# A Mamba block and a butterfly FFN on one core: state products in row halves, a decay formed from sums, and new orders in the first and the last unit

## The reference, cut to what matters

```python
x = x + ssm(layernorm(x), in_proj_w, conv_w, conv_b, x_proj_w, A_log, D, out_proj_w)
x = x + ffn(layernorm(x), W_exp, b_exp, up_weights, up_bias, down_weights, W_con, b_con, down_bias)

def ssm(x, ...):
    x_inner, z = split(x @ in_proj_w.T)              # 2 x 512 channels
    x_conv = silu(causal_conv4(x_inner) + conv_b)
    x_dbl = x_conv @ x_proj_w.T                      # 1 + 16 + 16 columns
    delta = softplus(x_dbl[..., 0]); B, C = x_dbl[..., 1:17], x_dbl[..., 17:]
    A = -exp(A_log)                                  # 16 rates
    # over the tokens t, for each of the 512 channels d and 16 states n
    h = h * exp(delta_t * A) + x_t[d] * delta_t * B_t[n];   y_t[d] = sum_n h[d, n] * C_t[n]
    return ((y + x_conv * D) * silu(z)) @ out_proj_w.T

def ffn(x, ...):                                     # 256 -> 1024 -> 256
    h = butterfly(x @ W_exp + b_exp, up_weights)     # 10 stages of 2x2 mixes
    h = butterfly(gelu(h + up_bias), down_weights)
    return h @ W_con + b_con + down_bias
```

## Time and profile before

| | |
|---|---|
| median of three runs | 568.49 us |
| lowest, highest | 566.38, 570.36 us |
| the profiled execution's own time | 569.59 us |
| its span, first to last instruction | 567.9 us |
| mean granted TensorE clock | 0.966 |
| TensorE matmuls busy | 528.9 us, 93% |
| VectorE, ScalarE, GpSimd busy | 72%, 54%, 19% |

### The profile page before, as it was taken

How to read it: one execution, slowest core, us unless ns; L and a number is a source line. 1 busy time by engine, 2 the same in 40 slices (tenths; PEclk the granted TensorE clock), 3 DMA queues, 4 the chain that set the end, 5 groups by cost and what they waited for, 6 DMA issues and landing times.

```text
span 567.9 us, 8152 instructions
## 1 busy us (share of the span) xinstructions
PE 528.9 (93%) x2996; PEld 430.3 (76%) x2996; DVE 409.6 (72%) x860; ACT 306.1 (54%) x526; POOL 109.5 (19%) x96
## 2 busy tenths in 40 slices
PE   3998899888999999999999999999999999699896
PEld 3766676776897779887888778877888788578886
DVE  4859999587983799468966799379946894575532
ACT  2876883865239622874268623962287417431342
POOL 4042100230201301050103120130105021411110
PEclk9986979799999999999999999999999999799999
DMA  8542311200012001210112001200021002100011
GB/s 244 97 27 3 80 35 38 76 2 2 23 52 74 4 2 48 66 39 2 37 41 74 0 9 68 71 8 1 5 73 38 0 2 74 41 1 0 6 34 37
DMA packets 42619, 21.75 MB, mean 38 GB/s; under 512 B 26419, under 2 KB 41011, under 8 KB 42580
## 3 DMA queue, kind: packets, MB, share of 16 engines
q1 hardware_dynamic: 39940, 17.57, 13.0%
q10 hardware_dynamic: 2640, 3.67, 2.3%
HBM read 16.78 MB, written 4.46 MB: 37 GB/s over the span
## 4 chain that ended last, share of the span: by engine, by line
PE 48%; DVE 20%; issue 12%; ACT 9%; SPq 6%; POOL 3%; DMA 0%; DVEq 0%; ACTq 0%; POOLq 0%
PE wide L711 12%; PE acc L844 9%; PE wide L833 7%; SPq L420 5%; PE wide L822 4%; DVE xc L1552 2%; DVE xc L1555 2%; POOL x1b_xn L598 2%; DVE state L1516 2%; DVE hid_low L1429 2%; PE wide L804 2%; PE small L731 2%; PE wide L811 2%; DVE xc L1412 2%; ACT L1054 2%
## 5 line engine op out<-in xcount | busy, mean ns | idle before, releaser
L1054 ACT ACTIVATE hid_f<-wide,bias_up 128x512 f32<-128x512 f32 x64 | 44.0, 687 | 162.0 <-PE wide L833 161.6
L1412 DVE SCALAR_TENSOR_TENSOR xc<-xi,taps,xc 128x512 f32<-128x512 f32 x96 | 87.0, 911 | 4.0 <-ACT xc L1085 1.7
L844 PE MATMUL acc<-w_down_high,hid_high 128*128 128x256 f32 x256 | 73.2, 286 | 5.6 <-DVE hid_low L1429 5.4
L844 PE MATMUL acc<-w_down_high,hid_low 128*128 128x256 f32 x256 | 71.9, 281 | 0.0
L844 PE MATMUL acc<-w_down_low,hid_high 128*128 128x256 f32 x256 | 71.9, 281 | 0.0
L1429 DVE TENSOR_TENSOR hid_low<-hid_f,hid_high 128x512 fp32r<-128x512 f32 x64 | 46.3, 725 | 29.8 <-ACT hid_high L1163 29.2
L833 PE MATMUL wide<-xnT_ln2T_high,w_up_high 128*128 128x512 f32 x128 | 55.4, 432 | 3.4 <-DVE xnT_ln2T_low L1423 1.8
L522 POOL TENSOR_TENSOR rstd<-var_eps,minus_half 128x4 f32<-128x4 f32 x16 | 19.1, 1192 | 202.8 <-DVE var_eps L1317 202.8
L711 PE MATMUL wide<-xnT_ln1T_high,w_in_high 128*128 128x512 f32 x128 | 56.5, 441 | 1.1 <-DVE xnT_ln1T_low L1423 1.0
L822 PE MATMUL wide<-w_out,xc 128*128 128x256 f32 x256 | 56.7, 379 | 0.3 <-DVE xc L1555 0.3
L844 PEld LDWEIGHTS acc<-w_down_high,hid_high 128*128 128x128 f32 x256 | 48.0, 188 | 11.2 <-issue 8.2
(11 more groups left out here) (185 smaller groups left out, 1054.6 us busy)
## 6 DMA issues: line engine op xcount, KB each, us to landing
x_res<-in_L_attn_x_dram SPq DMA_DIRECT2D x9, 512.0 KB, 3.5
c_near<-c_of_tokens SPq DMA_DIRECT2D x8, 512.0 KB
out_dram<-x1b_xn SPq DMA_DIRECT2D x8, 512.0 KB, 2.9
x_ln<-in_L_attn_x_dram SPq DMA_DIRECT2D x7, 512.0 KB, 3.6
xc<-in_L_attn_in_proj_w_dram ACTq DMA_DIRECT2D x2, 512.0 KB, 7.1
...
```

The costliest lines, as they stand in the source:

```text
L844: last = pe.matmul(acc[:, c, :], hid[h][:, j % HRING, c * P:(c + 1) * P], w_down[w][:, j, 0:DM], start=j == 0 and c % 2 == 0 and n == 0, s ...
L1054: ins = act.activation(out_ap, in_ap, how.pop("func"), **how)
L1412: ins = dve.scalar_tensor_tensor(xc[u % BATCH][:, e, :], xi[:, e, tap:tap + TILE], taps[:, e, tap:tap + 1], xc[u % BATCH][:, e, :], ALU.mu ...
```

## The change

- **State products in row halves.** A bank of y now holds 256 tokens of two channel groups. The product with `state` takes partitions 0 to 63 for the first 256 tokens and 64 to 127 for the others: eight products of 256 columns on 64 rows each in a unit of work, in place of four of 512 columns on 128 rows. `ssm_output(u, 0)` and `(u, 1)` are now parted by `up(3)` and `down(1)`; `gates` takes four half-width steps and two full ones for each pair.
- **Transposes.** The tokens of the x projection are turned by four transposes with the identity, and VectorE adds the two halves in the copy; before, products with `fold` did both.
- **Decay with sums ahead of rates.** `step_sums` also sums masked steps (32 more columns); VectorE multiplies them by the rates (`gap_w`), ScalarE takes the exponential in place (`exp_gaps`), GpSimd multiplies B by it (`weigh_b`, behind `place_c_block` and ahead of `diagonal_times_b`), TensorE transposes, and ScalarE copies to `b_hat` (`take_b_hat`). `gap_products`, `weigh_gaps` and VectorE's `weigh_b` go.
- **Order on the other engines.** VectorE makes `convolve(v, 1)` ahead of `diagonal_times_c` and `low_hidden(p, 0)` ahead of `assemble`. GpSimd's `residual_with_bias` moves from behind the gates to the head of the next unit. ScalarE loads the Gelu table before the first `gelu`.
- **Orders of phases 0 and 7.** In phase 0 the transposes of unit 1 and its input projections move ahead, GpSimd clears its tiles ahead of `rstd_of(1)`, and `low_parts(2)` moves ahead of `first_residual`. In phase 7 `up(6, 0..2)` come before `step_sums`.
- **Last unit in halves.** The last two `down` blocks, `final` and the store are made for 256 tokens at a time.

```diff
-    WIDE_ORDER += uses(("up", range(3)), of=phase - 1) + uses(("y", range(CB)), of=phase)
-    WIDE_ORDER += uses(("up", range(3, 5)), of=phase - 1) + uses(("out", range(2)), of=phase)
+    WIDE_ORDER += uses(("up", range(3)), of=phase - 1) + uses(("y", range(2)), of=phase)
+    WIDE_ORDER += uses(("up", [3]), of=phase - 1) + uses(("y", range(2, CB)), of=phase)
+    WIDE_ORDER += uses(("up", [4]), of=phase - 1) + uses(("out", range(2)), of=phase)
     WIDE_ORDER += uses(("up", range(5, HB)), of=phase - 1)
-    SMALL_ORDER += uses(("xtok", range(GR)), ("xdtok", [0]), of=phase)
-    SMALL_ORDER += uses(("ln1T", range(MB)), of=1) if phase == 0 else uses(("ln2T", range(MB)), of=phase - 1)
-    SMALL_ORDER += uses(("sums", [0]), ("gap", [0]), ("bd", [0]), ("ct", [0]), ("cbd", [0]), ("u", [0]), ("moff", [0]), of=phase)
+    SMALL_ORDER += uses(("xtok", range(GR)), of=phase) + (uses(("ln1T", range(MB)), of=1) if phase == 0 else [])
+    SMALL_ORDER += uses(("xdtok", [0]), of=phase) + uses(("ln2T", range(MB)), of=phase - 1)
+    SMALL_ORDER += uses(("sums", [0]), ("ct", [0]), ("cbd", [0]), ("u", [0]), ("bd", [0]), ("moff", [0]), of=phase)
     SMALL_ORDER += uses(("ln1T", range(MB)), of=phase + 2)
 ACC_ORDER = [("down", 0, u) for u in range(UNITS)]
...
+        steps_at = sb("steps_at", [P, GR + GR * NB])
+        delta, steps_before = steps_at[:, 0:GR], steps_at[:, GR:GR + GR * NB].rearrange("p (c j) -> p c j", j=NB)
...
+            def weigh_b(u):
+
+                wait(pool, gap_decays, u, 1)
+                wait(pool, b_masked, u, 1)
+                pool.tensor_tensor(bd_tok[:, :, :, :], bd_tok[:, :, :, :], gap_w[:, :, :, :], ALU.mult)\
+                    .then_inc(bd_ready.handle, 1)
...
-                weigh_gaps(u)
+                if u:
+                    residual_with_bias(u - 1)
                 mask_b(u)
                 diagonal_gaps(u)
                 place_c_block(u)
+                weigh_b(u)
                 diagonal_times_b(u)
                 if u + 2 < UNITS:
                     rstd_of(u + 2, 0, var1, rstd1)
-                if u:
-                    wait(pool, gated, u, CB)
-                    residual_with_bias(u - 1)
                 rstd_of(u, 1, var2, rstd2)
             residual_with_bias(UNITS - 1)
...
-                    last = pe.matmul(bank[:, c * P:c * P + XD], xdT[:, c * P:(c + 1) * P], fold[:, :], start=True, stop=True)
+                    last = pe.transpose(bank[:, c * P:(c + 1) * P], xdT[:, c * P:(c + 1) * P], ident[:, :])
...
-                    pe.matmul(bank[:, n * GR:(n + 1) * GR], mask[:, :], delta[:, :], start=True, stop=True)
-                pe.matmul(bank[:, 12:13], dA[:, :, :].rearrange(flat), ones[:, 0:1], start=True, stop=True)
-                mark_written(pe.matmul(bank[:, 16:16 + GR * BL], in_block[:, :], d_place[:, :, :].rearrange(flat),
...
+            def ssm_output(u, pair):
+
+                banks = [tile_of("y", 2 * pair + h, u) for h in range(2)]
+                for h in range(2):
+                    free(pe, u, "y", 2 * pair + h)
+                if pair == 0:
+                    read(pe, u, "moff", 0)
+                for q in range(2):
+                    g = 2 * pair + q
+                    for c in range(GR):
+                        at = q * HALF_TILE + c % 2 * P
+                        pe.matmul(banks[c // 2][:, at:at + P], x_tok[:, c, g * P:(g + 1) * P],
+                                  m_mat[:, c * P:(c + 1) * P], start=q == 0 and c % 2 == 0, stop=False,
+                                  skip_group_check=True)
+                if pair == 0:
+                    read(pe, u, "ct", 0)
+                    wait(pe, first_state, u, 1)
+                    wait(pe, states_ready, u, 1)
+                for q in range(2):
+                    g = 2 * pair + q
+                    for h in range(2):
+                        rows = slice(2 * SLOT * h, 2 * SLOT * (h + 1))
+                        last = pe.matmul(banks[h][:, q * HALF_TILE:(q + 1) * HALF_TILE],
+                                         state[u % BATCH][rows, g * P:(g + 1) * P],
+                                         c_startT[rows, h * HALF_TILE:(h + 1) * HALF_TILE],
+                                         start=False, stop=q == 1, skip_group_check=True)
+                        if q == 1:
+                            mark_written(last, "y", 2 * pair + h, u)
...
                 in_or_none(v, 2)
                 in_or_none(v, 3)
+                if v == UNITS:
+                    for j in range(3):
+                        up(p, j)
                 step_sums(u)
                 in_or_none(v, 4)
-                decayed_b(u)
...
                 down(p, 0)
-                ssm_output(u)
+                ssm_output(u, 0)
                 up(p, 3)
                 down(p, 1)
+                ssm_output(u, 1)
...
+                first, second = range(GR // 2), range(GR // 2, GR)
+                down(u, HB - 2, first)
+                down(u, HB - 1, first).then_inc(first_half_down, 1)
+                down(u, HB - 2, second)
+                down(u, HB - 1, second)
...
             def exp_gaps(u):
+                wait(act, gap_exponents, u, 1)
+                whole = gap_w[:, :, :, :].rearrange("p c j n -> p (c j n)")
+                act.activation(whole, whole, ACT.Exp).then_inc(gap_decays.handle, 1)
+
+            def take_b_hat(u):
                 written(act, u, "moff", 0, ago=1)
-                take(u, "gap", 0, b_hat[:, :], tile_of("gap", 0, u)[:, :], func=ACT.Exp)
+                take(u, "bd", 0, b_hat[:, :], tile_of("bd", 0, u)[:, :])
...
+                wait(dve, bd_ready, u, 1, ago=1)
+                dve.tensor_tensor(gap_w[:, :, :, :].rearrange("p c j n -> p (c j) n"),
+                                  bank[:, 12:12 + GR * NB].unsqueeze(2).to_broadcast([P, GR * NB, NS]),
+                                  rates[:, :].unsqueeze(1).to_broadcast([P, GR * NB, NS]), ALU.mult)\
+                    .then_inc(gap_exponents.handle, 1)
...
+            def gates(u, pair):
+
+                own = xc[u % BATCH]
+                if pair == 0:
                     wait(dve, z_ready, u, 1)
-                written(dve, u, "y", g)
-                mark_read(dve.scalar_tensor_tensor(y, y, skip[:, g:g + 1], tile_of("y", g, u)[:, :], ALU.mult, ALU.add),
-                          "y", g, u)
-                read(dve, u, "y", g)
-                dve.tensor_tensor(y, y, z[u % BATCH][:, g, :], ALU.mult).then_inc(gated.handle, 1)
+                for h in range(2):
+                    written(dve, u, "y", 2 * pair + h)
+                    tokens = slice(h * HALF_TILE, (h + 1) * HALF_TILE)
+                    for q in range(2):
+                        g = 2 * pair + q
+                        ins = dve.scalar_tensor_tensor(own[:, g, tokens], own[:, g, tokens], skip[:, g:g + 1],
+                                                       tile_of("y", 2 * pair + h, u)[:, q * HALF_TILE:(q + 1) * HALF_TILE],
+                                                       ALU.mult, ALU.add)
+                        if q:
+                            mark_read(ins, "y", 2 * pair + h, u)
+                        else:
+                            ins.then_inc(skipped.handle, 1)
...
                 take_sums(u)
                 weigh(u)
-                weigh_b(u)
                 beside("weighed")
                 if v < UNITS:
                     convolve(v, 0)
+                    convolve(v, 1)
                 diagonal_times_c(u)
                 sum_diagonal(u)
+                beside("summed")
+                low_hidden(p, 0)
                 assemble(u)
-                beside("assembled")
-                low_hidden(p, 0)
                 advance_state(u)
                 low_hidden(p, 1)
                 if r < UNITS:
                     first_stats(r)
-                gate(u, 0)
-                gate(u, 1)
+                gates(u, 0)
                 low_hidden(p, 2)
                 if r < UNITS:
                     first_normalise(r)
-                gate(u, 2)
-                gate(u, 3)
-                if v < UNITS:
-                    convolve(v, 1)
+                gates(u, 1)
                 low_hidden(p, 3)
                 if v < UNITS:
                     convolve(v, 2)
...
+            last, h = UNITS - 1, GR // 2
+            wait(dve, x1b_ready, last, 1)
+            dve.wait_ge(first_half_down, 1)
+            dve.tensor_tensor(x1b[:, 0:h, :], acc[:, 0:h, :], x1b[:, 0:h, :], ALU.add).then_inc(first_half_final, 1)
+            written(dve, last, "down", 0)
+            mark_read(dve.tensor_tensor(x1b[:, h:GR, :], acc[:, h:GR, :], x1b[:, h:GR, :], ALU.add), "down", 0, last)
```

207 lines of the change are left out of this document (93 added, 114 removed).

## The result

The changed kernel takes 583.35 us, the median of four runs (583.2 to 585.7); the kernel before took 568.36 beside it. The ratio is 1.028, with a 95% interval of 1.025 to 1.031: 15 us slower, where 569 was forecast and the range ended at 577. The profiled execution took 583.44 us with a span of 581.7, the one of before 569.59 with 567.9.

A forecast was written before the change was run, and what follows sets the result against it. It took TensorE to bound steady units, with VectorE and GpSimd taking over after the change. Terms -1.8 - 1.4 - 2.0 + 6.5 - 0.7 = +0.6 us on 568.5 gave 569.1, forecast 569, range 555 to 577.

The forecast's parts named there:

- TensorE as the bound, and VectorE taking over: Units 2 to 5: TensorE sheds 2.9 us, but VectorE and GpSimd then decide; 0.45 us saved each, -1.8 in all.
- the 0.43 us ahead of `step_sums`: Steady units: four transposes replace the token products of the x projection; this saving alone stays, 0.43 us a unit.
- The row halves: State products on TensorE: halves run side by side, 0.9 us a pair for 1.72, saving 1.6 us a unit.
- The bound of 3.2 us for a pair: State products: upper end for a pair if weight loads no longer hide and double; serial alone was 1.72 us.
- Units 0 and 1: First two units: two waits removed against added GpSimd product and halved gates; -2 us for both, bounds -6 and +2.
- Unit 7: Last unit: `up` blocks delay `step_sums` by 8.1 us and leave the scan's chain bare; +6.5 us, bounds +2 and +9.
- Unit 6: No statistics or normalising of a later unit, so TensorE decides again, apart from the later `m_mat`; -1.4 us.
- The tail: End of the last unit: halving saves 0.6 us of the first `final`, little of the second; -0.7 us, bounds 0 and -1.3.
- The rivals.: Three other outcomes: TensorE stays the bound, 555 us; row halves not side by side, 576; unit 7 loses nothing, 562.5.
- TensorE stays the bound: Rival, chance 0.22: weaker port exclusion, gates done 2 to 3 us sooner, units 2 to 5 save 2.9 each; 555 us.
- Serial row halves: Rival, chance 0.21: state-product halves don't run side by side, costing 0.8 us a pair; 576 us.
- A free unit 7: Rival, chance 0.11: unit 7 loses nothing, as the clock rises at once and the bare chain is shorter; 562.5 us.

The follow-up runs named there:

- the two orders put back: Changed kernel with the convolution's steps and the last unit's order as before, here also without the row halves: 577.0 us, ratio 1.014.
- Two edits that shortened a wait of TensorE there: Changed kernel, unit 0 only: first pair of gates ahead of short paths and statistics, 586.1 us; or y and state product in whole rows, 583.0 us.

## Why the prediction was wrong

**TensorE as the bound, and VectorE taking over** (steady units, -0.45 each forecast, 0 measured). The mechanism held on VectorE: its steps with two SBUF operands stand still beside GpSimd's products, the place of `diag` times c (12.2 forecast, 11.8 measured) and of the gates (30.5 and 30.1) came out, and the convolution steps beside GpSimd took 1.6 to 2.8 us (three of the six, the other three followed at 0.75). Two steps failed.

First, the 0.43 us ahead of `step_sums` were to stay, because `softplus` had time to spare for the residual that GpSimd now makes beside it. It had not enough: `step_sums` came 0.09 us later than before. With the residual put back it came 0.30 us sooner, and with the transposes alone it starts at 10.75 us, the whole 0.4 sooner than before.

Second, TensorE was to be at `out_projection` at 29 and to wait there for the gates. It came at 30.7, after them. From y to `out_projection` it took 14.1 us where 12.2 were counted: 0.6 are the state products (next term), and 1.2 are two waits inside, for the first gates (0.97) and for the state (0.21), both put at nothing. A third wait, 1.58 us at the first `down`, stands ahead of y. The wait for the gates is not the row halves' own: in unit 4 it is 1.3 us in the changed kernel with whole rows (and the two orders put back), and there is none in the kernel before with the halves alone.

**The row halves** (1.6 us a unit forecast). Side by side was right, at 1.06 us a pair for 0.9. The halves alone take TensorE from y to `out_projection` in 12.81 us for 14.23 before, and 0.42 of that is the old wait, so the term is 1.0 a unit; TensorE's busy time fell by 0.8. The bound of 3.2 us for a pair can't be redone from its rows (1.72 and eight doubled loads of 0.11 are 3.5); nothing hangs on it. The Trainium skill, "TensorEngine Tiling (Array Packing)", Key Properties, has a drain at each change of the tiling mode. Fully side by side a pair would take 0.86 us, and it takes 1.06 with both changes; the first state product also starts 0.21 us after the last product with `m_mat`, where it was 0.11. So this trace leaves about 0.3 us at most for the two drains of a pair.

**Units 0 and 1** (-2 forecast, +6.0 measured). This term failed by its sign and is the largest miss, 8.0 of the 13.2 us between the sums. I had credited two waits that the new orders take away and bounded the loss at +2. The row halves alone lost 4.6 us in the two units, the decay alone 2.5, the first phase's order some 2 (1.6 and 2.7 in two comparisons of profiled executions). They don't add: the residual's new place alone gains 1.4 us there, and with the halves beside it the two units lose 1.2. Which of them makes the 6 us in the changed kernel is not settled. In five executions here the same code of unit 0 took 73.7, 74.0, 74.9, 75.5 and 77.4 us at a granted clock of 0.91, 0.88, 0.86, 0.84 and 0.78; the kernel before took 69.7 at 0.85, so the loss of unit 0 is not the clock, but a difference of a microsecond between two runs can be. Two edits that shortened a wait of TensorE there did not lower the median. That VectorE (64.24 of 74.90 us busy) holds the unit as much as TensorE (61.78) fits this; a price by part is not shown.

**Unit 7** (+6.5 forecast, +8.8 measured). Right in mechanism, under-sized in its parts. `step_sums` came 9.3 us later than before by the unit's clock, for 8.1: the low parts 0.85 us later than counted, the `up` blocks 6.6 for 6.3. The bare chain to y took 16.0 us for 15.3, so y starts 7.8 us later, for 5.9. And the 1.6 us for the state products were some 1.0. Undoing the order gives 7.1 us back. The other 1.7 fit the decay and the row halves alone, which change unit 7 by +2.9 and -0.8 us; I had costed the decay at nothing there.

**Unit 6** (-1.4 forecast, +0.3 measured). TensorE did not decide again: with the convolution's order back it takes 58.2 us, 1.5 less than before. That is the whole of the forecast gain of 1.4, and the moved block stood in front of it.

**The tail** was forecast at -0.7 and measured at -1.0: right.

**The rivals.** TensorE stays the bound (555 us) fell as to the changed kernel; with the convolution back, the waits left are 1.5 us. Serial row halves fell: 1.06 us. A free unit 7 fell. The slower side came from edits that I had costed alone and at little, not from any of the three.

**The residual's place,** costed as neutral, is the one part that pays only with another: nothing alone, -9.0 us beside the row halves, and in the changed kernel, with the convolution's order moved, a loss of 2.5. The loss of 0.3 us in a steady unit there is the later `step_sums`; the 1.3 us of unit 1 were not traced further.
